# A graph layer on one core: the order in which VectorE makes a chunk's payload parts, with the second half split from the last part

## The reference

```python
# layer 0: u = x
dx   = maximum(edge_attr_2[:, 0], 1e-6)
diff = (u[dst] - u[src]) / dx[:, None]                 # the payload of an edge
d1   = segment_sum(diff, dst) - segment_sum(diff, src)
S    = segment_sum(edge_attr_2[:, 1] / dx, dst)        # the slope
x1   = layernorm(x + u - dt * (u * d1 + g * S))
# layer 1: mean of edge attributes over the destination
mean = segment_sum(edge_attr_16, dst) / counts(dst)
out  = layernorm(x1 + mean)
```

## Time and profile before

| | us |
|---|---|
| median of 3 runs | 4494.73 (4491.13 to 4495.12) |
| the profiled execution, its own time | 4491.46 |
| span of its trace | 4489.6 |
| PE busy | 4396.0 (98%) |
| DVE busy | 3896.7 (87%) |
| POOL busy | 3316.7 (74%) |
| ACT busy | 1431.9 (32%) |

### The profile page before, as it was taken

How to read it: one execution, slowest core, us unless ns; L and a number is a source line. 1 busy time by engine, 2 the same in 40 slices (tenths; PEclk the granted TensorE clock), 3 DMA queues, 4 the chain that set the end, 5 groups by cost and what they waited for, 6 DMA issues and landing times. The chain is left out here.

```text
span 4489.6 us, 74222 instructions
## 1 busy us (share of the span) xinstructions
PE 4396.0 (98%) x31379; PEld 1159.0 (26%) x12630; DVE 3896.7 (87%) x8730; ACT 1431.9 (32%) x1018; POOL 3316.7 (74%) x3133
## 2 busy tenths in 40 slices
PE   4999999999999999999999999999999999999997
PEld 1222222222222222222222222222222222222222
DVE  7988888888888888888888888888888888888887
ACT  4333333333333333333333333333333333333320
POOL 7777777777777777777777777777777777777760
PEclk9999999999999999999999999999999999999998
DMA  3111111111111111111111111111111111111110
GB/s 94 35 35 35 43 37 35 35 35 42 37 35 35 36 42 37 35 35 41 39 35 35 35 43 37 35 35 35 43 37 35 35 35 42 37 35 35 36 31 8
DMA packets 210292, 167.80 MB, mean 37 GB/s; under 512 B 124651, under 2 KB 193775, under 8 KB 210025
## 3 DMA queue, kind: packets, MB, share of 16 engines
q1 hardware_dynamic: 109798, 139.79, 9.9%
q0 software_dynamic: 100000, 25.80, 6.6%
q10 hardware_dynamic: 476, 2.01, 0.1%
HBM read 164.55 MB, written 2.81 MB: 37 GB/s over the span
## 5 line engine op out<-in xcount | busy, mean ns | idle before, releaser
L662 PE MATMUL ps_src<-hi_hot,spread_lo 128*128 128x392 bf16 (+1 forms) x18750 | 4114.8, 328 | 0.0
L436 POOL DMA_INDIRECT x_src<-in_x_dram,src_i x3125 | 3311.7, 1060 | 1039.9 <-issue 906.0
L1018 DVE TENSOR_SCALAR hi_hot<-col_h,hi_f,scale 128x1564 bf16<-128x1564 f16 x3125 | 2161.3, 711 | 24.4 <-PE ps_src L662 23.2
L657 PE MATMUL ps_src<-hi_hot,spread_lo 128*128 128x392 bf16 x6250 | 2048.4, 328 | 11.4 <-DVE hi_hot L1018 9.3
L657 PEld LDWEIGHTS ps_src<-hi_hot,spread_lo 128*128 128x128 f16 x6250 | 616.0, 99 | 1718.2 <-issue 1383.6
L537 ACT ACTIVATE nodes_mem<-rel_all,row_neg 128x3200 bf16<-128x3200 f16 x125 | 370.3, 2962 | 1507.1 <-PE ps_x L599 1505.0
L610 PEld LDWEIGHTS ps_w<-dst_hots,parts 128*102 128x102 bf16 x3125 | 391.3, 126 | 939.4 <-issue 901.4
L997 DVE TENSOR_TENSOR spread_lo<-spread_lo,halves 128x640 f16<-128x640 f16 x1250 | 603.3, 491 | 12.6 <-PE ps_src L662 12.4
L599 PE MATMUL ps_x<-xwin,nodes_mem 112*128 112x48 bf16 x3125 | 579.9, 188 | 20.4 <-DVE parts L926 13.5
L610 PE MATMUL ps_w<-dst_hots,parts 128*102 128x112 bf16 x3125 | 499.5, 213 | 0.0
L599 PEld LDWEIGHTS ps_x<-xwin,nodes_mem 112*128 112x128 bf16 x3125 | 302.4, 98 | 601.2 <-issue 563.5
(11 more groups left out here) (120 smaller groups left out, 1164.2 us busy)
## 6 DMA issues: line engine op xcount, KB each, us to landing
rel_all<-rel_d SPq DMA_DIRECT2D x125, 800.0 KB
x_src<-in_x_dram,src_i POOLq DMA_INDIRECT x3125
a<-in_edge_attr_dram SPq DMA_DIRECT2D x125, 200.0 KB, 2.4
a<-in_edge_attr_dram SPq DMA_DIRECT2D x125, 25.0 KB
src_i<-in_src_dram SPq DMA_DIRECT2D x125, 12.5 KB, 1.7
dst_i<-in_dst_dram SPq DMA_DIRECT2D x125, 12.5 KB, 1.7
xwin<-xparts_d SPq DMA_DIRECT2D x125, 10.5 KB
dst_sum<-in_dst_dram SPq DMA_DIRECT2D x1, 1400.0 KB
```

Of the source, the lines that this page charges most:

```text
L436: nc.gpsimd.indirect_dma_start(x_src[:, b, j * F:(j + 1) * F], None, x[:, :], bass.IndirectOffsetOnAxis(ap=src_i[:, b, j:j + 1], axis=0)). ...
L657: return nc.tensor.matmul(out_bank, weights, moving, start=False, stop=stop)
L662: return nc.tensor.add_instruction(mybir.InstMatmult(name=nc.get_next_instruction_name(), engine=pe.engine, start_tensor_calc=False, stop_ ...
L1018: v.tensor_scalar(hi_hot[:, slot(j), 0:HOT], col_h[:, 0:HOT], hi_f[:, b, j:j + 1], scale[:, b, j:j + 1], ALU.is_equal, ALU.mult).then_inc( ...
```

## The change

`PIECES` is written anew for tiles 3 to 12, and the piece `parts` is cut in two: `half1` (the second half) and `parts` (the third part of the payload). `half1` has a semaphore of its own, `half1_ready`, instead of a count in `dve_step` that was waited for right away. ACT makes the payload's second part before the first half. PE waits for `half1_ready` too, at tile 11 and once before the loop. `SECOND_PIECES` has `left` ahead of `scale`, and `parts` ahead of `half1`.

```diff
-        PIECES = {2: ["x_of_dst"], 3: ["x_in", "rel2"], 4: ["dst_hot"], 5: ["diff"], 6: ["attr_left", "dst_hot"], 7: ["pay", "lo"],
-                  8: ["dst_hot"], 9: ["scale", "dst_hot"], 10: ["scaled", "attr_parts"], 11: ["left", "dst_hot"], 12: ["parts"], 14: ["dst_rel"],
+        PIECES = {2: ["x_of_dst"], 3: ["x_in", "rel2", "attr_left"], 4: ["dst_hot", "attr_parts"], 5: ["diff", "dst_hot"], 6: ["pay", "dst_hot"], 7: ["lo", "left"],
+                  8: ["scale", "parts"], 9: ["scaled", "dst_hot"], 10: ["half1", "dst_hot"], 14: ["dst_rel"],
...
-        SECOND_PIECES = {0: ["attr_left", "rel2"] + ["dst_hot"] * 5 + ["attr_parts", "dst_rel", "x_of_dst", "x_in", "lo", "diff", "pay", "scale", "scaled", "left", "parts",
+        SECOND_PIECES = {0: ["attr_left", "rel2"] + ["dst_hot"] * 5 + ["attr_parts", "dst_rel", "x_of_dst", "x_in", "lo", "diff", "pay", "left", "scale", "scaled", "parts", "half1",
                             "slope"] + ["spread"] * 6}
...
-        A_STEPS, B_STEPS, W_STEPS = 2, 20, 1
+        A_STEPS, B_STEPS, W_STEPS = 2, 19, 1
...
                 nc.scalar.copy(parts[:, :, 0, 0:F + 1], pay[:, :, :]).then_inc(part0_ready, 1)
+                act.wait_ge(left_ready, n + 1)
+                nc.scalar.copy(parts[:, :, 1, 0:F + 1], left[:, :, :]).then_inc(part1_ready, 1)
                 act.wait_ge(scaled_ready, n + 1)
...
                 nc.scalar.copy(halves[:, :, 0, :], scaled[:, :, :]).then_inc(half0_ready, 1)
-                act.wait_ge(left_ready, n + 1)
-                nc.scalar.copy(parts[:, :, 1, 0:F + 1], left[:, :, :]).then_inc(part1_ready, 1)
...
                     if j == BANK_AT and begin:
+                        pe.wait_ge(half1_ready, c + 2)
                         pe.wait_ge(parts_ready, c + 2)
...
             pe.wait_ge(parts_ready, 1)
+            pe.wait_ge(half1_ready, 1)
             x_of_dst(1)
...
-                if piece == "parts":
+                if piece == "half1":
                     dve.wait_ge(scaled_ready, n + 1)
                     dve.wait_ge(half0_ready, n + 1)
-                    step(v.tensor_tensor(halves[:, :, 1, :], scaled, halves[:, :, 0, :], ALU.subtract))
-                    done["half1"] = count[0]
-                    settle_here()
+                    v.tensor_tensor(halves[:, :, 1, :], scaled, halves[:, :, 0, :], ALU.subtract).then_inc(half1_ready, 1)
+                if piece == "parts":
                     dve.wait_ge(left_ready, n + 1)
                     dve.wait_ge(part1_ready, n + 1)
...
                     if at == 0:
-                        settle_here("half1")
+                        dve.wait_ge(half1_ready, n + 1)
```

1 line of the change is left out of this document (added).

## The result

| | before | changed |
|---|---|---|
| median | 4492.47 us (6 runs, 4491.13 to 4495.12) | 4528.61 us (6 runs, 4526.94 to 4530.30) |
| ratio | | 1.0080, 95% interval [1.0070, 1.0091] |
| span of the profiled execution | 4489.6 | 4526.0 |

The account below looks back on a forecast made before the run. PE's own matmuls were taken to bound the kernel; 0 in the loop, 0.1 us or so in the start and 0 at the end left the four runs' middle, 4493.1, so 4493 us, range 4489 to 4499.

Parts of the forecast that it names:

- What bounds the kernel: Whole loop: stages are as long as PE's own matmuls, and PE has no wait between 220 and 4380 us.
- The slack at tiles 8 and 10: Hots of tiles 9 and 11 still ready 1.25 and 0.99 us before PE (3.97 and 2.97 before); loop loss 0.
- the other queues: SP, POOL and ACT beside DVE's loop: loads two chunks ahead, POOL's gathers in unchanged order; no cost expected.
- The rule on the two sides of SBUF: VectorE's two-port modes shut GpSimd out from writing descriptors, so hots near gathers could slow them; shares the slow rival's 0.05.
- The four waits for ACT: DVE's `attr_left`, attributes' third part, last part and second half: no wait expected; tightest has 0.4 us to spare.
- the wait that goes: DVE's `settle_here` wait for the second half before the last part: 0.034 us each, 125 times, worth 0.
- the wait that is added on PE: `half1_ready`, once per stage: taken as 0, upper end 5 us; as a rival 4498, chance 0.06.
- The start: First two stages: waits for parts become waits for hots; sum 0.1 us or so.
- The slow rival: VectorE comes late for tile 10 in every stage, once delays exceed 0.99 us together; up to 4613 us, chance 0.05.
- price line: The slow rival's cost: 0.07 us of excess per stage is 9 us, 0.2 us is 24 us, giving 4517.

Follow-up runs that it names:

- e5: Changed kernel with `attr_left` and `attr_parts` moved back behind `diff` (tiles 6 and 7), the payload's new order kept; 4495.16 us, ratio 1.0005.
- e11: Changed kernel with the attributes' third part alone moved back from tile 4 to tile 7, between `lo` and `left`; 4495.29 us, ratio 1.0008.
- e12: Changed kernel with the attributes' third part alone moved from tile 4 to tile 5, right behind `diff`; 4495.23 us, ratio 1.0006.
- e8: Changed kernel with 24 gathers per chunk in place of 25, which leaves work out; 4489.76 us, ratio 0.9994.
- e13: Kernel before with `attr_left` at tile 3, an extra unused f32 subtraction at tile 4 and a `settle_here` before the gather's wait; 4498.77 us, one run.
- e18: e13 with one operand of the extra subtraction in PSUM in place of SBUF; 4493.09 us, ratio 1.0002.
- e6: Kernel before with only the attributes' two pieces moved, `attr_left` to tile 3 and `attr_parts` to tile 4; 4494.08 us, ratio 1.0004.
- e9: Kernel before with two extra unused subtractions, at tiles 3 and 4, all operands in SBUF, and a `settle_here` before the gather's wait; 4493.87 us, ratio 1.0004.
- e16: Changed kernel with tile 4's two pieces in the other order, the attributes' third part ahead of `dst_hot`; 4493.44 us, ratio 1.0001.

## Why the prediction was wrong

*What bounds the kernel.* Right for before: e5, e11 and e12 show that PE's 34.99 us stand as long as DVE has its gather in time.

*The slack at tiles 8 and 10.* The working was right within 0.5 us. Forecast 1.25 and 0.99 us; where nobody waits for the gather (e12), 1.56 and 1.44. What used it up is a wait for POOL. In the changed kernel the subtraction of u[src] starts 2.80 us into PE's stage, in e8, with the same order on DVE and no such wait, 1.10: 1.70 us later. The hot of tile 11 had 1.44 - 0.06 = 1.38 us to give, which leaves 0.32 us for PE to wait; the stage is 0.29 us longer.

*The step that failed* is that on the other queues: "POOL's gathers ... their order is as it was", and in the rival, "since the same instructions run per stage, I see nothing that would make it 1.3 us per stage". The mean of a gather is no constant of POOL. In the trace of before, 270 gathers ran while DVE had no instruction under way, and each took 0.94 or 0.95 us; the other 2599 took 1.07 in the mean. It hangs on where DVE's instructions lie. What the runs showed in place of that step: with the attributes' third part at tile 4, the last gather of a chunk takes 2.14 us instead of 0.94 in every stage, its data come 1.40 us after that, DVE stands 1.53 us for them, and the subtraction starts 1.70 us late, more than the 1.56 and 1.44 us of slack that the payload's new order has left. One instruction moved away (e12) or a gather fewer (e8) ends it. POOL had 34.99 - 34.18 = 0.8 us to spare in a stage, less than the 1.2 us of that one gather. It could have been seen: the earlier trace rows give a mean of 1060 ns, and the earlier trace rows a gather of 0.94. The difference, 0.12 x 25 = 3 us per stage, was a hold already. I weighed 33.7 against 35.0 and called the rest safe, without asking how the 3 us come about. The four waits of DVE that I went through were those for ACT; the one for the gather, 6.40 us in the first stage of before, was not among them.

*The rule on the two sides of SBUF.* The prediction named the Trainium skill's page SBUF — State Buffer, section SBUF: two separate sides, for this rival and gave it part of 5%. The same section of the Trainium skill says more than I used: that the pair of ports is held for a whole instruction, and that a VectorE instruction with two SBUF inputs counts too, against a GpSimd instruction that reads SBUF. e13 against e18 agrees with that (2.14 against 1.65 us, one operand changed). The hold lasts over several instructions of DVE here, though, up to the end of the next hot. No run shows what part of the gather reads SBUF.

*The four waits for ACT, the wait that goes, the wait that is added on PE.* Right: none shows in the changed kernel's loop, and e5, which has the added wait, is at 1.0005.

*The start.* The trade of parts' waits for hots' was right in kind. Its sizes and its place weren't: the first gather that DVE waits for came 1.10 us later (72.56 against 71.46), and the second stage's wait of 1.23 us stands at tile 8, where the forecast had 0.05 us at tile 10. PE began the third stage 0.65 us later than before, where the forecast had 0.1 us or so. PE's wait for parts ahead of the loop is 13.3 us in place of 13.5, as estimated, but its first stage began 0.26 us later all the same (59.86 against 59.60).

*The slow rival.* Right in what one sees (hots late for tiles 8 and 10 in every stage), wrong in its first cause, a wait for ACT. Its price line, an excess of 0.2 us for 24 us, agrees with the 0.29 us and 36 us here, and so does its reason, that DVE begins each stage at a fixed point of PE's and the stage grows by the excess.

What stays open: why a gather starts at just this point in nearly every stage of the changed kernel and of e6 (119 and 118 of 119), and in 19 of e9. A release puts the next gather at a fixed distance from DVE's instruction, so that the two could lock together. That POOL keeps PE's pace to 0.02 us in e16 without waiting for anything fits that; what makes it fall into step, or get free as in e12, is argued, not shown. Also open is why the changed kernel never slips one gather ahead, as e6 does in its ninth stage, and whether it would stay free if it once had a lead: no run of it with all gathers had one.
